# A routed feed-forward block on one core: the second matrix and the combination turned over

## The reference

```python
capacity = max(1, int(Sz * CAP_FACTOR / E) + 1)            # 1024 * 2 / 8 + 1 = 257
scores = softmax(einsum('bsd,ed->bse', x, router_w))        # 8 experts
gate_vals, sel_idx = top_k(swapaxes(scores, 1, 2), capacity)
tokens = x[b_idx, sel_idx]                                  # (2, 8, 257, 128)
h = gelu(einsum('becd,edh->bech', tokens, w1) + b1)         # 512 hidden
y = einsum('bech,ehd->becd', h, w2) + b2
out = zeros_like(x).at[b_idx, sel_idx].add(y * gate_vals[..., None])
```

## Time and profile before

| | |
|---|---|
| median of 3 runs | 1246.82 us (1246.41 to 1247.45) |
| profiled execution | 1245.78 us, span 1244.0 us |
| PE, PEld | 1112.8 us (89%), 806.7 us (65%) |
| DVE, ACT, POOL | 647.0 (52%), 518.2 (42%), 302.1 us (24%) |
| `combine`, L1451 | 1024 products, 169.9 us |
| `output`, L1425 | 1152 products, 168.2 us |
| `hidden`, L1417 | 384 products, 93.3 us |
| products of constants in the feed-forwards, L409 | 334, 52.9 us |

### The profile page before, as it was taken

The page is one execution under the profiler, slowest core; times in us unless marked ns, Lnnn a source line. Parts: engine busy times, 40 slices in busy tenths (PEclk is TensorE's granted clock), DMA queues, the critical chain, the costliest instruction groups (busy, mean ns, idle before and its releaser), DMA issues. The chain is left out here.

```text
span 1244.0 us, 19477 instructions
## 1 busy us (share of the span) xinstructions
PE 1112.8 (89%) x7507; PEld 806.7 (65%) x7507; DVE 647.0 (52%) x1298; ACT 518.2 (42%) x1120; POOL 302.1 (24%) x566
## 2 busy tenths in 40 slices
PE   3889999999875999999998899999987679999998
PEld 2555566565553899999974334444435469999998
DVE  5867677776365433321145877777754734332221
ACT  2346666666610444222113466666663044432220
POOL 1532466533202223110004122222221042311000
PEclk9989999999977699755568899999999869985555
DMA  3833232211171000000005410000004400000001
GB/s 84 256 92 117 64 109 63 70 42 53 52 249 68 14 15 17 13 7 3 1 0 153 118 61 28 27 27 2 1 2 140 184 19 20 15 11 10 5 1 34
DMA packets 45805, 69.82 MB, mean 56 GB/s; under 512 B 12073, under 2 KB 32337, under 8 KB 45330
## 3 DMA queue, kind: packets, MB, share of 16 engines
q1 hardware_dynamic: 38322, 59.44, 15.6%
q0 software_dynamic: 2176, 4.48, 1.5%
q10 hardware_dynamic: 5216, 4.66, 1.3%
HBM read 42.40 MB, written 25.03 MB: 54 GB/s over the span
## 5 line engine op out<-in xcount | busy, mean ns | idle before, releaser
L1051 ACT ACTIVATE b_pt<-b_banks 128x512 f32<-128x512 f32 (+1 forms) x320 | 154.7, 559 | 102.0 <-PE b_banks L965 101.7
L1451 PE MATMUL f_banks<-f_ys,f_spread 128*128 128x128 f32 x1024 | 169.9, 343 | 0.0
L1599 DVE TENSOR_TENSOR f_hr<-f_h,f_hr 128x516 fp32r<-128x516 f32 x64 | 44.6, 696 | 240.7 <-ACT f_hr L1574 240.7
L1451 PEld LDWEIGHTS f_banks<-f_ys,f_spread 128*128 128x128 f32 x1024 | 169.4, 262 | 0.2
L1425 PE MATMUL f_banks<-f_w2r,f_hr 128*128 128x128 f32 (+1 forms) x1152 | 168.2, 313 | 0.0
L1425 PEld LDWEIGHTS f_banks<-f_w2r,f_hr 128*128 128x128 f32 (+1 forms) x1152 | 159.5, 206 | 3.4
L1302 POOL DMA_INDIRECT f_xg<-scratch_table,f_index x64 | 68.0, 1063 | 358.7 <-DVE f_ys L1616 229.6
L1074 DVE TENSOR_REDUCE a_mlate<-a_banks 128x2 f32<-128x1024 f32 (+3 forms) x120 | 124.9, 1079 | 51.2 <-PE a_banks L903 32.7
L1074 DVE TENSOR_REDUCE b_mlate<-b_banks 128x2 f32<-128x1024 f32 (+3 forms) x120 | 126.0, 1081 | 36.4 <-PE b_banks L903 18.3
L1568 ACT ACTIVATE f_h<-f_banks,b_t 128x258 f32<-128x258 f32 x128 | 58.9, 475 | 182.1 <-PE f_banks L1417 180.5
L965 PE MATMUL a_banks<-a_q,a_k 121*128 121x512 f32 (+3 forms) x384 | 117.5, 384 | 5.3 <-DMA a_q<-a_mt 4.4
(11 more groups left out here) (233 smaller groups left out, 1428.4 us busy)
## 6 DMA issues: line engine op xcount, KB each, us to landing
scratch_w<-a_tab SPq DMA_DIRECT2D x16, 512.0 KB, 3.0
f_w1r<-scratch_w SPq DMA_DIRECT2D x16, 512.0 KB, 7.2
f_w2r<-scratch_w SPq DMA_DIRECT2D x16, 512.0 KB, 8.0
a_rot<-in_w SPq DMA_DIRECT2D x16, 256.0 KB, 3.7
a_q<-scratch_q SPq DMA_DIRECT2D x8, 384.0 KB
a_k<-scratch_k SPq DMA_DIRECT2D x8, 384.0 KB
scratch_q<-b_q_hl SPq DMA_DIRECT2D x24, 128.0 KB, 2.8
b_q<-scratch_q SPq DMA_DIRECT2D x32, 96.0 KB
```

Source lines behind the costliest of these rows:

```text
L1051: act.activation(pt[at % NPT][:, h, 0:cols], st[u % NST][:, 0:cols], ACT.Exp, scale=scale).then_inc(exp_done, 1)
L1451: last = pe.matmul(sum_ps[t], spread[q % 2][:, c, t * P:(t + 1) * P], ys[q % 2][part][:, c, :], start=(e == 0 and t % TPC == 0 and c == 0 ...
L1599: dve.tensor_tensor(hr[q % 2][1][:, span, :], h[q % 2][:, span, :], hr[q % 2][0][:, span, :].bitcast(F32), ALU.subtract).then_inc(h_low, 1)
```

## The change

In words:

- **Second matrix turned over.** In `output` the weights now stand still and 258 columns of `h` pass, as in `hidden`: 12 products a round, in two halves of 6, giving y with its 128 features on the rows. `take_y` (ACT) copies that out with `b2` as a bias, `turn_y` (PE) turns it back in two transposes, and `high_y` and `low_y` scale it and split it as before, one round later than now. The left-over column of all 8 experts is turned once a batch (`turn_left_y`), so the row's DMA is gone. Left-over rows of x are turned once a batch too (`turn_left`).
- **Combination turned over.** `ys` stands still and 512 columns of the one-hot pass: 8 products a round. Sums then have features on the rows; `take_sum` copies them and `turn_sum` turns them back, 4 transposes for each half of a batch, before `add`.
- **No products of constants** in the search, the marks, the places and the first gather.
- The comparisons of both batches in a search step are one instruction, on scores that are copied three times beforehand (`scores3`).
- Five gather buffers instead of four, `spread_left` is one buffer and is made at the sixth expert, `h`, the sums and `rank` lie in memory that already exists, and `one_hot(q)` runs one round earlier.
- `constants` turns `b2` on PE instead of splitting it and moving the low part by DMA.

```diff
-WB, GB = NE, 4
+WB, GB = NE, 5
...
-                sp.wait_ge(b2_split, 2)
-                sp.dma_start(m.b2_r[1:2, :].bitcast(F32), b2_low[:, :].bitcast(F32)).then_inc(moved, 16)
-                sp.wait_ge(moved, 16)
...
+                pe.transpose(small[:, 2 * P:2 * P + NE], b2[:, :], m.ident[0:NE, 0:NE]).then_inc(turned, 1)
...
-        "logits": [(8, 6, 3, 3), (4, 4, 3, 3)], "search": 6, "marks": 20, "places": 5, "gather": 15}
+        "logits": [(8, 6, 3, 3), (4, 4, 3, 3)], "search": 0, "marks": 0, "places": 0, "gather": 0}
...
-        def product(q, to, columns, ones):
-            e = q % NE
-            for j in range(HB):
-                for i, (wp, hp) in enumerate(((0, 0), (0, 1), (1, 0))):
-                    pe.matmul(to, hr[q % 2][hp][:, j, columns], w2r[e][:, wp, j * D:(j + 1) * D],
-                              start=(j == 0 and i == 0), stop=False)
-            return pe.matmul(to, ones, m.b2_r[:, e * D:(e + 1) * D], start=False, stop=True)
...
+            for j in range(first, first + 2):
+                for i, (wp, hp) in enumerate(((0, 0), (0, 1), (1, 0))):
+                    last = pe.matmul(yt_ps, w2r[e][:, wp, j * D:(j + 1) * D], hr[q % 2][hp][:, j, :],
+                                     start=(j == 0 and i == 0), stop=(j == HB - 1 and i == 2))
...
+        def turn_y(q):
+            b, e = divmod(q, NE)
+            pe.wait_ge(y_taken, q + 1)
+            if q:
+                pe.wait_ge(gated, q)
+            if b and e == 0:
+                pe.wait_ge(left_gated, b)
+            for c in range(2):
+                last = pe.transpose(y_ps[:, c, :], y_t[:, e, c * P:(c + 1) * P], m.ident[:, :])
+            last.then_inc(y_turned, 1)
...
-            for t in range(QT):
-                for c in range(2):
-                    for part in range(2):
-                        last = pe.matmul(sum_ps[t], spread[q % 2][:, c, t * P:(t + 1) * P], ys[q % 2][part][:, c, :],
...
+            for c in range(2):
+                for part in range(2):
+                    for i in range(2):
+                        last = pe.matmul(sum_ps[i], ys[q % 2][part][:, c, :], spread[q % 2][:, c, i * CH:(i + 1) * CH],
...
+        def take_y(q):
+            b, e = divmod(q, NE)
+            act.wait_ge(y_mm, q + 1)
+            if q == NE:
+                act.wait_ge(left_turned, 1)
+            elif q > NE:
+                act.wait_ge(y_turned, q - NE + 1)
+            act.activation(y_t[:, e, :], yt_ps, ACT.Identity, bias=m.b2_t[:, e:e + 1]).then_inc(y_taken, 1)
...
+            three = lambda t: t.rearrange("p b n t e -> p (b n) t e")
+            dve.tensor_tensor(three(mask[:, :, :, :, :]), three(scores3[:, :, :, :, :]),
...
+            if q >= 2:
+                low_y(q - 2)
             low(q, 0)
...
             low(q, 2)
-            if q:
-                low_y(q - 1)
-                one_hot(q - 1)
+            one_hot(q)
```

More of the change, by code:

```diff
@@ L1292, in sync @@
             sp.wait_ge(stored, 16 * NCH)
-        for i in range(2):
-            sp.wait_ge(left_moved[i], 16 * (NQ // 2))
     def gpsimd(pool):
@@ L1401, in turn_x, with turn_left @@
             pe.wait_ge(g_in[q % GB], 32 * (q // GB + 1))
+            for i in range(2):
+                last = pe.transpose(xt_ps[:, i * P:(i + 1) * P], xg[q % GB][:, i, 0:D], m.ident[:, :])
+            last.then_inc(x_turned, 1)
+        def turn_left(b):
             pe.wait_ge(left_in[b], 16)
[L1403 to L1405 removed]
+            pe.transpose(xl_ps, xl[b][:, 0:D], m.ident[0:NE, 0:NE]).then_inc(left_mm, 1)
         def hidden(q, j):
@@ L1458, in combine_left, with turn_sum @@
             pe.wait_ge(left_gated, b + 1)
-            for t in range(QT):
+            for i in range(2):
                 for part in range(2):
-                    last = pe.matmul(sum_ps[t], spread_left[b][:, t * P:(t + 1) * P], ys_left[part][:, :], start=False,
+                    last = pe.matmul(sum_ps[i], ys_left[part][:, :], spread_left[:, i * CH:(i + 1) * CH], start=False,
                                      stop=(part == 1), skip_group_check=True)
-                if t % TPC == TPC - 1:
-                    last.then_inc(summed, 1)
+                last.then_inc(summed, 1)
+        def turn_sum(c):
+            pe.wait_ge(sum_taken, c + 1)
+            if c in (1, 2):
+                pe.wait_ge(added, c)
+            for i in range(TPC):
+                at = (c % 2 * TPC + i) * P
+                last = pe.transpose(t_ps[c][:, i * P:(i + 1) * P], sum_t[:, at:at + P], m.ident[:, :])
+            last.then_inc(sum_turned, 1)
         if projected:
@@ L1487, in tensor @@
                 turn_x(q + 1)
+            if q + 1 == NE:
+                turn_left(1)
+            if q >= 2:
+                turn_y(q - 2)
             hidden(q, 0)
             hidden(q, 1)
+            if q == NE + 1:
+                turn_left_y(0)
             if q == NE + 2:
@@ L1503, in tensor @@
                 indices(1)
+        turn_y(NQ - 2)
         output(NQ - 1, 0)
-        output(NQ - 1, 1)
+        output(NQ - 1, 2)
         combine(NQ - 2)
+        turn_y(NQ - 1)
         combine(NQ - 1)
+        turn_left_y(1)
         combine_left(1)
+        turn_sum(2)
+        turn_sum(3)
     def scalar(act):
@@ L1563, in scalar @@
                 high_x(q + 1)
+            if q >= 2:
+                high_y(q - 2)
             for j in range(HB):
@@ L1574, in scalar @@
                     act.activation(hr[q % 2][0][:, j - 1:j + 1, :], h[q % 2][:, j - 1:j + 1, :], ACT.Copy).then_inc(h_high, 1)
+                if q == NE + 2 and j == 1:
+                    take_sum(0)
+                    take_sum(1)
             if q:
-                high_y(q - 1)
+                take_y(q - 1)
             if q == PLACES - 1:
@@ L1580, in scalar @@
                 high_left(0)
+        high_y(NQ - 2)
+        take_y(NQ - 1)
         high_y(NQ - 1)
         high_left(1)
+        take_sum(2)
+        take_sum(3)
     def vector(dve):
@@ L1593, in low_x, with low_left_x @@
             dve.wait_ge(x_high, q + 1)
-            dve.tensor_tensor(xs[q % 2][1][:, :], xt_ps, xs[q % 2][0][:, :].bitcast(F32), ALU.subtract).then_inc(x_split, 1)
+            b, e = divmod(q, NE)
+            dve.tensor_tensor(xs[1][:, e, 0:FULL], xt_ps, xs[0][:, e, 0:FULL].bitcast(F32), ALU.subtract).then_inc(x_split, 1)
+        def low_left_x(b):
+            dve.wait_ge(left_x_high, 2 * (b + 1))
+            for i in range(2):
+                column = lambda part: xs[part][:, :, FULL + i:FULL + i + 1].rearrange("p e o -> p (e o)")
+                last = dve.tensor_tensor(column(1), xl_ps, column(0).bitcast(F32), ALU.subtract)
+            last.then_inc(left_x, 1)
         def low(q, first):
@@ L1731, in copy_index @@
             dve.tensor_copy(local_left[:, b:b + 1], index_left_ps[:, 0:1]).then_inc(index_ready, 1)
+        for b in range(B):
+            link(dve.tensor_copy(scores3[:, b, :, :, :], scores[:, b:b + 1, :, :].to_broadcast([P, 3, QT, NE])))
         link(dve.tensor_tensor(trial[:, :, :, :], over_trials(found[:, :, :]), steps(0), ALU.bitwise_or))
@@ L1762, in vector @@
                 low_left(0)
+        low_y(NQ - 2)
         low_y(NQ - 1)
-        one_hot(NQ - 1)
         low_left(1)
-        add(1)
+        add(2)
+        add(3)
     stage = Stage()
```

166 lines of the change are left out of this document (92 added, 74 removed).

## The result

The changed kernel takes 992.91 us (median of four runs, 989.49 to 993.11) against 1247.13 for the kernel before: a ratio of 0.7948, with a 95% interval of 0.7921 to 0.7975. The direction was right, but 1023 with a range from 1005 was 30 us too slow. The profiled execution took 993.11, its span 991.4, so 252.6 of span are gone.

The account below looks back on a forecast made before the run. PE's list of products and its clock were taken as the bound. A stage summed to 133.1 us (23.0, 1.3, 86.1, 5.7, 3, 14) instead of 244.0, twice; with search +1.1 a stage and setup -3.0, 1245.78 became 1023; range 1005 to 1065.

Parts of the forecast that it names:

- New round at 2.4 GHz: PE's products in one expert round, summed from old trace prices: 6.1 us against 10.15 before.
- the 0.05 that I added to 6.1: Expert round on PE: 6.15 us taken for a round whose products sum to 6.1, with 6.0 and 8 as ends.
- the 131 ns: Combination: the skill's price of a sustained 512-column product, making it 1.05 us; the prediction used the trace's 0.23 each instead.
- the front: Start of a stage, first gather to the products of the second list: 24.7 us before, 23.0 forecast.
- the list's products: The second list's products on PE, once a stage: 1.3 us.
- the extras: Once a stage: transposes and products of sums, PE's waits, second indices and left transposes: 5.7 us, from 3 to 10.
- the low clock: Around combine_left: perhaps one fall of the clock, two rounds at half speed, 3 us a stage.
- the tail: End of a stage, the last output, combinations, transposes, hand-overs and addition: 13.8 us, 14 with the clock.
- Search and first list: Search steps, merged comparison, score copies and lists without products of constants: net +1.1 us a stage, from -3 to +3.
- one fall and a return within a round or two: Clock after combine_left: falls perhaps once, then returns, expected from each round's eight 512-column products.
- The ring of waits: Rival, chance 0.10: take_y, turn_y, high_y, low_y and one_hot don't fit; rounds of 7.4 us instead of 6.15, total 1058.
- the second batch low: Rival, chance 0.10: the clock falls at combine_left and stays low, 30 us more a stage, total 1083.

Follow-up runs that it names:

- two_rows: The changed kernel with one product of 2 rows and 258 columns more behind each six of the second matrix; 1021.62 us, 0.8175 of the kernel before.
- all_rows: The changed kernel with one product of all 128 rows and 258 columns more behind each six of the second matrix; 997.24 us, 0.7990 of the kernel before.
- out_128: The changed kernel with the second matrix's twelve products of 258 columns divided into 24 of 128 and 130; 1029.91 us, 0.8247 of the kernel before.
- no_bias: The kernel before without its three bias products of 2 rows a round; 1099.58 us in the profiled execution, 1139.97 in a second one without a trace.
- Constants_back: The changed kernel with the products of constants put back in the search and around the first list; median 985.40 us.
- comb_128: The changed kernel with the combination's eight products of 512 columns divided into 32 of 128; 1058.88 us, 0.8479 of the kernel before.
- both_128: The changed kernel with second matrix in 24 products of 128 and 130 columns and combination in 32 of 128; 1123.66 us, 0.8991 of the kernel before.

## Why the prediction was wrong

The mechanism was right: PE was the bound and stayed it, the round's length and the clock set the stage, the clock rose in the products of the second list, fell once around combine_left and came back, this last for another reason than I gave. What failed is the step "New round at 2.4 GHz", whose sum of 6.1 measured 5.19 in the round shown and 5.17 in the next. Its terms:

| | forecast | measured |
|---|---|---|
| four transposes | 0.68 | 0.36 |
| first matrix | 1.77 | 1.53 |
| second matrix | 1.80 | 1.45 |
| combination | 1.88 | 1.85 |

With the 0.05 that I added to 6.1, that is 1.0 a round, and 14 rounds in two stages are 27 of the 30 us. I took the prices of products of 258 columns from a loop in which they stand between bias products of 2 rows and trains of 128 columns, and carried them into a loop that has neither. Two_rows, all_rows and out_128 show what was in them: of the 0.47 for three, 0.36 is the products and 0.11 the 2-row product directly ahead of them, which two_rows has in full without any short product. Behind a train of 128 columns instead it is 0.06 (out_128, no_bias); the two do not add up. The transposes held something like it: 0.34 stood ahead of a product of 8 rows; in the changed kernel's own trace two of them take 0.31 where such a product follows (920.65), and 0.21 to 0.22 in the rounds around it. No run takes that apart further.

The combination's eight products of 512 columns took 0.23 us each, as in the earlier trace rows; the 131 ns that the prediction named from the Trainium skill ("TensorE: Matmul & The Clock Gate", Back-to-back issue gap) don't show in this trace.

The other terms of a stage: the front 21.7 (870.26 to 891.95; forecast 23.0), the list's products 1.7 (1.3), the extras and the low clock 9.8 (82.2 from 893.61 to 975.81, less 14 x 5.17; forecast 5.7 + 3), the tail 12.5 (14). The waits at turn_left_y and turn_y(8) were 1.20 and 1.63, forecast 1.1 and 1.6. Together they are off by 1.3; the rounds are off by 13.7.

Search and first list: 42.17 before (955.06 to 997.23) and 43.48 after (826.78 to 870.26), +1.3 in the second stage, +1.5 in the first, forecast +1.1. Constants_back divides it: 2.0 for the constants, so the merged comparison and its copies together gained about 0.7; I had 0.6 (1.2 less 0.6 for the copies).

The clock: one fall and a return within a round or two was what I forecast (some 7 us), but the reason (eight products of 512 columns) fell with comb_128, so this was right by luck. Of the rivals none came. The ring of waits is absent, in rounds 3 to 8 PE has no gap; the second batch low is what the kernel before shows to its end, and both_128 for 48 us.

The bound that I left out stood in the trace. Behind a train of twelve products of 128 columns, which begins at 1045.22, comes this row:

```profile
1046.61 0.32 PE L1427 MATMUL f_banks<-b_r,ones_r 2*128 2x128 f32 x1
```

So the trains of 128 columns ran at 0.116 (12 in 1.39), the groups of 258 at 0.138 (six) and 0.157 (three): a fifth to a third more for twice the columns, so columns were not what set either price. The lower end for a product was its share of the 512 columns that took 0.23: 0.116 for 258 and 0.058 for a transpose. With these a round is 4 x 0.058 + 24 x 0.116 + 1.88 = 4.9, and 28 rounds by 1.25 less make 988; the range should have reached that far.

## What to carry to other kernels

A price read from start to start holds what the neighbours leave uncovered; before it is carried into a new list, ask which neighbour goes, and take as lower bound the price per column of the longest products in the trace. Look for products with few rows (a bias as a product of ones, a handful of left-over rows): each cost as much as three or four full ones here, and in the old list, together with short products, they went with a clock at half for half of the loop. When a clock falls and stays, remove the smallest suspects first: three products in a round moved 1247 to 1100, and to 1140 in a second execution. And look at every stage of a trace before a fall, or none, is put down to an edit: out_128 shows one of each.

## What was not expected of the hardware

- A product of 2 rows among those of 128 takes 0.31 us, and 0.20 more from the products around it; the same with 128 rows takes 0.12.
- Trains of 128 columns ran at 0.1075 (out_128, 12 in 1.29) to 0.110 a product (comb_128, 32 in 3.52), and those of 258 at 0.121 (6 in 0.73, the changed kernel): at 2.4 GHz twice the columns cost some 0.01 us more.
- The granted clock, once down, came back after 3 to 7 us in the changed kernel, comb_128 and no_bias (in its one trace), after 34 and 48 in both_128 and not within 128 in the kernel before, there with PE busy throughout.
